# Up products of the first seven expert tiles: plain fp32 from whole copies in place of a high-low split

## The chip, the cores and the metric

One core of one Trainium2 chip runs the whole kernel. The metric is the device time of one execution in microseconds (us). Three runs of the kernel before gave 521.81, 521.89 and 523.43 us; their median, 521.89 us, is what the changed kernel is held against.

## The reference, cut to what matters

A decoder layer over 8 batches of 256 tokens of width 128: causal attention with 16 heads, a retention step, and a mixture of 12 experts of which each token takes 3. The change touches only the experts' up product:

```python
gate_logits = x @ Wg                                  # 12 experts, the 3 largest are taken
h = gelu(einsum('bsd,edh->ebsh', x, Wup) + bup)       # 128 -> 512, this product changes
y = einsum('ebsh,ehd->ebsd', h, Wdown) + bdown        # 512 -> 128
x = x + sum over the 3 chosen experts of weight * y
```

## The kernel before, in words

**Batches.** Attention and retention go batch by batch in a software pipeline over TensorE, VectorE, ScalarE and GpSimd. Each batch's tokens are routed (functions `route_a`, `choose`, `route_b`, `route_c` on VectorE, L1271 to L1318) and GpSimd scatters them by indirect DMA, six transfers of one batch (`send`, L533), into a DRAM table in which every expert owns a region.

**Tiles.** The experts' work is cut into 35 tiles, each for one expert, in one order on every engine. Tiles 0 to 6 (`n < EARLY`) have 256 tokens and are made only of tokens of the first six batches, so they may start before the last batches are routed. Tiles 7 to 23 (up to `BIG`) have 256 tokens and need all batches; tiles 24 to 34 have 128 tokens.

**One tile.** SP loads its rows (`load`, L372 to L388). TensorE transposes them into a PSUM bank (`turn_tokens`, L1034). ScalarE copies the expert's up weights (`up_high`, L761) and the transposed tokens (`tokens_high`, L766). TensorE forms four up products of 128 hidden units each (`up`, L1037 to L1055), ScalarE applies gelu (L746), TensorE forms the down product (`down`, L1074), VectorE adds the bias and scales by the routing weight (`results`, L1512 and L1515), GpSimd scatters the rows (L600).

**The split.** Tiles 0 to 23 take the up product in the type fp32r: ScalarE's copies are the high parts, VectorE forms the low parts of tokens and weights (`tokens`, L1483 and L1496), and each of the four products is three matmuls of 256 columns (`split_product`, L798 to L802: high by high, high by low, low by high). Tiles 24 to 34 take plain fp32 (L1046), with the weights copied by VectorE (L1493) and the tokens by ScalarE. In the profile a plain fp32 matmul stands as two records, an fp32r matmul as one.

**Order around the change.** It is written out by hand. TensorE: `turn(7)` with `turn_tokens(0)` inside it, `weigh(6)`, `counts(6)`, `weigh(7)`, `turn_tokens(1)`, the output projection of the last batch, `up(0)`, two state products, `turn_tokens(2)`, `down(0)`, `up(1)`, two state products, `turn_tokens(3)`, `down(1)`, `up(2)`, the logits of the last batch, `down(2)`, `counts(7)`, and from tile 3 on `turn_tokens(n+1)`, `up(n)`, `down(n-1)`. VectorE has `tokens(0)` between `choose` and the scaling of the attention output (`scale_out`, L1205), then `route_b`, `route_c` of batch 6 and the copy `pad_row` (L1527), and puts `tokens(1)`, `tokens(2)`, `tokens(3)`, `results(0)`, `results(1)` between the steps of the last batch's norms and routing; `late_plan` (L1440) comes after `results(2)`, `small_units` after `results(6)`, `small_rows` after `results(7)`. `turn_tokens(n)` waits until VectorE has both low parts of tile n-1, since they read the same bank.

**SP and GpSimd.** After `pad_row` SP runs a loop of 12 stores (L394 to L396) that write padding rows behind each expert's tokens. GpSimd may scatter the last batch (`begin(7)`, L537 to L542) only when all 12 have landed (`padded`), and SP may load tile 7 (L385 to L388) only when that scatter has landed (`dispatched`). SP's loads of tiles 0 to 5 stand ahead of the padding loop, those from tile 6 on behind it.

Of the kernel before, what the change touches and what calls it, by code (L numbers as in the profile page):

```python
# [12 lines left out]
ACT = mybir.ActivationFunctionType  # L13
AX = mybir.AxisListType

P = 128
# [3 lines left out]
H, DH = 16, 64  # L20
# [4 lines left out]
E, HID, TOPK = 12, 512, 3  # L25
HC = HID // P
N = B * S
SLOTS = 256
# [3 lines left out]
EARLY = -(-((B - 2) * S * TOPK - E * (SLOTS - 1)) // SLOTS)  # L32
SMALL = E - 1
LATE = -(-(UNITS - HALVES * EARLY - SMALL) // HALVES)
BIG = EARLY + LATE
TILES = BIG + SMALL
DEPTH = 6
# [43 lines left out]
def decoder(nc, x, ctx, norm_w, wq, wkv, wout, wg, f_wg, f_wup, f_bup, f_wdown, f_bdown, tables, out):  # L81
    with ExitStack() as stack:
        def sb(name, shape, dt=F32):
            return stack.enter_context(nc.sbuf_tensor(name, shape, dt))
# [4 lines left out]
        def sem(name):  # L89
            return stack.enter_context(nc.semaphore(name))  # L90
# [3 lines left out]
        wq_sb = sb("wq_sb", [P, H * DH])  # L94
# [32 lines left out]
        v_sb = sb("v_sb", [P, T, H, DH])  # L127
# [80 lines left out]
        wup_all = sb("wup_all", [P, E, HID])  # L208
# [13 lines left out]
        wup_hi = sb("wup_hi", [P, 2, HID], F32R)  # L222
        wup_lo = sb("wup_lo", [P, 2, HID], F32R)
        xgT_hi = sb("xgT_hi", [P, 2, SLOTS], F32R)
        xgT_lo = sb("xgT_lo", [P, 2, SLOTS], F32R)
        xg = sb("xg", [P, DEPTH, HALVES, ROW])
        sb("rest_of_early", [P, 512])
        y3 = [a[:, 0:TOPK * FOUT * D].rearrange("p (k n d) -> p k n d", k=TOPK, n=FOUT) for a in (
            wkv_sb, y_in,
            p_sb[:, :, :, :].rearrange("p a h k -> p (a h k)"), pT[:, :, :, :].rearrange("p a h k -> p (a h k)"))]  # L230
# [11 lines left out]
        ffn_up = [[sc[:, 0, :], sc[:, 2, :]], tb]  # L242
        ffn_T = sc[:, 1, :]

        def halves(n):

            return HALVES if n < BIG else 1

        def results_before(n):

            return 16 * sum(halves(m) for m in range(n % DEPTH, n, DEPTH))

        def wup_one(n):

            return v_sb[:, n % 2, 0:HID // DH, :].rearrange("p h d -> p (h d)")

        def xgT_one(n):
            return v_sb[:, n % 2, HID // DH:HID // DH + P // DH, :].rearrange("p h d -> p (h d)")

        def place_of(n):  # L260

            if n < EARLY:
                return first_plan, n
            return (plan, n - EARLY) if n < BIG else (small_plan, n - BIG)
# [17 lines left out]
        def score_place(w, h):  # L282
# [27 lines left out]
        f_T, f_hi, f_w, f_xg, f_up, f_gelu, f_dn, f_y, f_out = (  # L310
            sem(n) for n in ("f_T", "f_hi", "f_w", "f_xg", "f_up", "f_gelu", "f_dn", "f_y", "f_out"))
# [12 lines left out]
        def wait(eng, s, value):  # L324
            if not isinstance(value, int) or value > 0:
                eng.wait_ge(s, value)
# [22 lines left out]
        def _(sp):  # L349
# [22 lines left out]
            def load(n):  # L372
                u = n % DEPTH
                table, k = place_of(n)
                if n >= DEPTH:

                    sp.wait_ge(f_row, n - DEPTH + 1)
                if n - DEPTH >= BIG:
                    sp.wait_ge(f_T, n - DEPTH + 1)
                r = sp.value_load(table[0:1, 0, k:k + 1], min_val=0, max_val=E * CAP)  # L380
                if n == 0:

                    sp.wait_ge(pe_Z, B * PAIRS)
                    sp.wait_ge(dispatched, (1 + (B - 2) * T * TOPK) * 16)
                if n == EARLY:  # L385

                    sp.wait_ge(dispatched, (1 + B * T * TOPK) * 16)
                sp.dma_start(xg[:, u, 0:halves(n), :], xs[bass.ds(r, halves(n) * P), :].rearrange("(a p) w -> p a w", p=P)).then_inc(ld_e[u], 16)  # L388

            sp.wait_ge(v_first, 1)  # L390
            for n in range(DEPTH):
                load(n)
# [4 lines left out]
            for n in range(DEPTH, EARLY):  # L397
                load(n)
# [12 lines left out]
            for c in range(NT // FOUT):  # L411
                for k in range(TOPK):
                    n = slice(c * FOUT, (c + 1) * FOUT)
                    sp.dma_start(y3[c][:, k, :, :], y_v[:, k, n, :]).then_inc(ld_y[c], 16)
            out_v = out.rearrange("b (t p) d -> p (b t) d", p=P)
            for c in range(NT // FOUT):
                n = slice(c * FOUT, (c + 1) * FOUT)
# [206 lines left out]
        def _(act):  # L624
# [113 lines left out]
            expert = {}  # L738
# [11 lines left out]
            def up_high(n):  # L750
                table, k = place_of(n)
                if n == BIG:
                    act.wait_ge(v_plan, 2)
                if n == 0:
                    act.wait_ge(v_first, 1)
                    act.wait_ge(ld_up, 16)
                if n == EARLY:
                    act.wait_ge(v_plan, 1)
                expert[n] = act.value_load(table[0:1, 1, k:k + 1], min_val=0, max_val=E - 1)
                if n < BIG:  # L760
                    act.activation(wup_hi[:, n % 2, :], wup_all[:, bass.ds(expert[n], 1), :].rearrange("p a n -> p (a n)"), ACT.Copy).then_inc(f_w, 1)  # L761

            def tokens_high(n):
                act.wait_ge(f_T, n + 1)
                to = xgT_hi[:, n % 2, :] if n < BIG else xgT_one(n)
                act.activation(to, ffn_T[:, 0:halves(n) * P], ACT.Copy).then_inc(f_hi, 1)  # L766

            def tile(n):
                if n + 1 < TILES:
# [2 lines left out]
                gelu(n)  # L772

            up_high(0)
            tokens_high(0)
            pT_out(B - 1, PAIRS - 1)
# [11 lines left out]
        def _(pe):  # L788
# [9 lines left out]
            def split_product(o, lhs, rhs, last):  # L798

                for n, (l, m) in enumerate(((0, 0), (0, 1), (1, 0))):  # L800
                    ins = pe.matmul(o, lhs[l], rhs[m], start=(n == 0), stop=(last and n == 2), skip_group_check=True)  # L801
                return ins  # L802
# [223 lines left out]
            def turn_tokens(n):  # L1026
                u = n % DEPTH
                pe.wait_ge(ld_e[u], (n // DEPTH + 1) * 16)
                if n > BIG:
                    pe.wait_ge(f_hi, n)  # L1030
                else:
                    wait(pe, f_xg, n)
                for a in range(halves(n)):
                    ins = pe.transpose(ffn_T[:, a * P:(a + 1) * P], xg[:, u, a, 0:D], ident[:, :])  # L1034
                ins.then_inc(f_T, 1)

            def up(n):  # L1037
                pe.wait_ge(f_xg, n + 1)
                if n >= BIG:
                    pe.wait_ge(f_hi, n + 1)  # L1040

                wait(pe, f_gelu, 2 * (n - 1))
                for k in range(HC):
                    c = slice(k * P, (k + 1) * P)
                    if n >= BIG:
                        ins = pe.matmul(ffn_up[n % 2][k // 2][:, (k % 2) * P:(k % 2 + 1) * P], wup_one(n)[:, c], xgT_one(n),  # L1046
                                        start=True, stop=True, skip_group_check=True)
                        if k % 2:
                            ins.then_inc(f_up, 1)
                        continue  # L1050
                    ins = split_product(ffn_up[n % 2][k // 2][:, (k % 2) * SLOTS:(k % 2 + 1) * SLOTS],
                                        (wup_hi[:, n % 2, c], wup_lo[:, n % 2, c]),
                                        (xgT_hi[:, n % 2, :], xgT_lo[:, n % 2, :]), True)
                    if k % 2:
                        ins.then_inc(f_up, 1)  # L1055
# [55 lines left out]
        def _(dve):  # L1111
# [364 lines left out]
            expert = {}  # L1476

            def tokens(n):
                u = n % DEPTH
                table, k = place_of(n)  # L1480
                if n < BIG:
                    dve.wait_ge(f_hi, n + 1)
                    dve.tensor_tensor(xgT_lo[:, n % 2, :], ffn_T[:, 0:SLOTS], xgT_hi[:, n % 2, :], ALU.subtract)  # L1483
                if n == 0:
                    dve.wait_ge(v_first, 1)
                if n == EARLY:
                    dve.wait_ge(v_plan, 1)
                if n == BIG:
                    dve.wait_ge(v_plan, 2)
                expert[n] = dve.value_load(table[0:1, 1, k:k + 1], min_val=0, max_val=E - 1)  # L1490
                if n >= BIG:
                    dve.wait_ge(f_up, 2 * (n - 1))
                    dve.tensor_copy(wup_one(n), wup_all[:, bass.ds(expert[n], 1), :].rearrange("p a n -> p (a n)")).then_inc(f_xg, 1)  # L1493
                else:
                    dve.wait_ge(f_w, n + 1)
                    dve.tensor_tensor(wup_lo[:, n % 2, :], wup_all[:, bass.ds(expert[n], 1), :].rearrange("p a n -> p (a n)"), wup_hi[:, n % 2, :], ALU.subtract).then_inc(f_xg, 1)  # L1496

                if n >= DEPTH:
                    dve.wait_ge(scattered[u], results_before(n))
                a = slice(0, halves(n))  # L1500
                if n >= BIG:
                    dve.wait_ge(ld_e[u], (n // DEPTH + 1) * 16)
                dve.tensor_copy(row_i[:, u, a], xg[:, u, a, D].bitcast(I32))
                dve.tensor_copy(weight[:, u, a], xg[:, u, a, D + 1]).then_inc(f_row, 1)
# [69 lines left out]
            for c in range(NT // FOUT):  # L1574
                dve.wait_ge(ld_y[c], 16 * TOPK)
                n = slice(c * FOUT, (c + 1) * FOUT)
                for k in range(TOPK):
                    ins = dve.tensor_tensor(x_all[:, n, :], x_all[:, n, :], y3[c][:, k, :, :], ALU.add)
# [25 lines left out]
```

## Time and profile before

| what | value |
|---|---|
| median of three runs | 521.89 us (521.81 to 523.43) |
| the profiled execution's own time | 523.74 us |
| its span in the profile | 522.0 us |
[...]
| TensorE busy | 457.5 us, 88% |
| VectorE busy | 393.2 us, 75% |
| ScalarE busy | 329.3 us, 63% |
| GpSimd busy | 256.1 us, 49% |

The profiled execution took 1.74 us around its span (start and end that the profile does not cover). It is 1.85 us above the median of the plain runs and near the highest of them. The expert tiles lie in the last 150 us of the span.

### The profile page before, as it was taken

How to read it: one execution, taken by the hardware profiler on the slowest of the kernel's cores; microseconds unless marked ns; L12 is line 12 of the kernel's file. 1: busy time of each engine (PE TensorE's matmuls, PEld its weight loads, DVE VectorE, ACT ScalarE, POOL GpSimd, SP SyncE). 2: the span in 40 equal slices, each digit the busy share in tenths (PEclk: the TensorE clock that was granted, in tenths of full speed). 3: DMA queues.
4: the chain of work that ended last, by engine and by line, in shares of the span. 5: the costliest groups of instructions: out<-in, count | busy, mean ns of one | idle time of the engine just before them, and what ended most of it. 6: DMA issues, size and time to landing. Idle time of an engine off the chain costs nothing.

```text
span 522.0 us, 12401 instructions
## 1 busy us (share of the span) xinstructions
PE 457.5 (88%) x3540; PEld 374.1 (72%) x3540; DVE 393.2 (75%) x1359; ACT 329.3 (63%) x1001; POOL 256.1 (49%) x398
## 2 busy tenths in 40 slices
PE   1689998999999999999999999976697798999980
PEld 1467786877777678687777767854466688999980
DVE  4755477988888888798888888889688766665556
ACT  3558865875776686687577668643445565776660
POOL 3400005157355535726735653575175764666861
PEclk9989999999999999999999999998798898999995
DMA  8990000000000000000000000001045242222248
GB/s 268 367 225 1 1 0 3 1 16 15 10 7 18 15 0 22 13 5 15 15 10 9 19 12 0 22 17 48 20 143 156 68 107 56 74 71 62 63 112 214
DMA packets 40803, 30.06 MB, mean 58 GB/s; under 512 B 3795, under 2 KB 36999, under 8 KB 40768
## 3 DMA queue, kind: packets, MB, share of 16 engines
q1 hardware_dynamic: 36864, 22.63, 15.5%
q0 software_dynamic: 3472, 6.49, 4.0%
q10 hardware_dynamic: 432, 0.53, 0.4%
q8 instruction: 16, 0.26, 0.2%
q14 instruction: 19, 0.16, 0.1%
HBM read 18.91 MB, written 11.44 MB: 58 GB/s over the span
## 4 chain that ended last, share of the span: by engine, by line
PE 52%; DVE 18%; ACT 8%; issue 8%; SPq 5%; POOL 5%; DMA 3%; DVEq 0%; ACTq 0%; POOLq 0%
PE zb L801 8%; PE sc L840 6%; PE ob L869 6%; PE xb L918 4%; PE zb L1074 3%; PE ob L1074 3%; PE xb L943 3%; PE sc L801 2%; PE tb_a L801 2%; ACT pT L667 2%; PE tb_a L853 2%; PE tb_b L853 2%; PE sc L834 2%; DVE nmx L1187 2%; ACT p_sb L660 2%
## 5 line engine op out<-in xcount | busy, mean ns | idle before, releaser
L651 ACT ACTIVATE qk<-zb 128x512 f32<-128x512 f32 x64 | 38.2, 597 | 66.9 <-PE zb L801 66.9
L520 POOL TENSOR_TENSOR spare_p<-tri 128x1 f32<-128x1 f32 x71 | 14.8, 209 | 125.3 <-DVE xn L1268 67.4
L600 POOL DMA_INDIRECT results_by_token<-y_sb,row_i x59 | 60.3, 1022 | 22.3 <-issue 21.8
L658 ACT ACTIVATE p_sb<-sc,nmx 128x128 f32<-128x128 f32 x128 | 47.1, 368 | 33.9 <-DVE nmx L1187 33.5
L660 ACT ACTIVATE p_sb<-sc,nmx 128x256 f32<-128x256 f32 x128 | 61.0, 476 | 0.0
L840 PE MATMUL sc<-qk 64*128 64x256 f32 (+1 forms) x512 | 60.4, 356 | 0.2 <-ACT qk L651 0.2
L869 PE MATMUL ob<-pT,v_sb 128*64 128x256 f32 (+1 forms) x512 | 58.2, 350 | 1.3 <-DVE oT L1205 1.3
L840 PEld LDWEIGHTS sc<-qk 64*128 64x128 f32 x512 | 45.1, 190 | 15.6 <-issue 10.1
L533 POOL DMA_INDIRECT tokens_by_expert<-packed,slot_i x48 | 48.2, 1005 | 8.6 <-issue 7.4
L1205 DVE TENSOR_TENSOR oT<-ob,pT 128x256 f32<-128x256 f32 x64 | 26.9, 420 | 27.1 <-PE ob L869 27.1
L869 PEld LDWEIGHTS ob<-pT,v_sb 128*64 128x64 f32 x512 | 32.3, 141 | 20.8 <-issue 11.2
L1187 DVE TENSOR_REDUCE nmx<-sc 128x2 f32<-128x512 f32 x64 | 43.5, 680 | 0.0
L1200 DVE TENSOR_TENSOR rg<-rr,gate 128x256 f32<-128x256 f32 x64 | 38.8, 606 | 2.2
L667 ACT ACTIVATE pT<-tb_b 128x512 f32<-128x512 f32 x64 | 39.8, 622 | 0.0
L667 ACT ACTIVATE pT<-tb_a 128x512 f32<-128x512 f32 x64 | 39.1, 612 | 0.0
L801 PE MATMUL zb<-xT_hi,wqk_hi 128*128 128x256 f32 x112 | 36.6, 326 | 1.3 <-ACT xN_hi L639 1.3
L853 PE MATMUL tb_a<-ident,p_sb 128*128 128x128 f32 x192 | 32.0, 276 | 2.2 <-ACT pT L667 2.2
L506 POOL TENSOR_TENSOR sum<-prod 128x256 f32<-128x256 f32 x30 | 21.9, 729 | 24.4 <-DVE prod L1250 24.3
L473 POOL TENSOR_TENSOR kq<-xn,tab 128x256 f32<-128x256 f32 x8 | 5.8, 722 | 55.8 <-DVE xn L1221 55.7
L1074 PE MATMUL zb<-wdn_all,hT 128*128 x248 | 32.3, 285 | 0.7 <-ACT hT L746 0.7
L746 ACT ACTIVATE hT<-sc,bup_sb 128x256 f32<-128x256 f32 (+1 forms) x72 | 25.9, 438 | 10.0 <-PE sc L801 7.8
L853 PE MATMUL tb_b<-ident,p_sb 128*128 128x128 f32 x192 | 31.8, 275 | 0.0
(294 smaller groups left out, 1375.4 us busy)
## 6 DMA issues: line engine op xcount, KB each, us to landing
xg<-tokens_by_expert SPq DMA_DIRECT2D x24, 130.0 KB, 2.2
tokens_by_expert<-padding SPq DMA_DIRECT2D x12, 260.0 KB
wup_all<-in_L_ffn_Wup SPq DMA_DIRECT2D x1, 3072.0 KB, 14.4
wdn_all<-in_L_ffn_Wdown SPq DMA_DIRECT2D x12, 256.0 KB, 5.7
wkv_sb<-in_L_attn_Wkv SPq DMA_DIRECT2D x2, 512.0 KB, 6.5
ctx_b<-in_ctx SPq DMA_DIRECT2D x8, 128.0 KB, 2.1
out<-x_all SPq DMA_DIRECT2D x4, 256.0 KB, 3.3
results_by_token<-y_sb,row_i POOLq DMA_INDIRECT x59
```

Source lines behind the costliest of these rows:

```text
L533: pool.indirect_dma_start(out=xs, out_offset=bass.IndirectOffsetOnAxis(ap=slot_i[:, t, k:k + 1], axis=0), in_=packed[:, t, k, :], in_offse ...
L600: pool.indirect_dma_start(out=ys, out_offset=bass.IndirectOffsetOnAxis(ap=row_i[:, u, a:a + 1], axis=0), in_=y_sb[:, u, a, :], in_offset=None,
L658: act.activation(p_sb[:, w, h, 0:P], sc[:, k, S:S + P], ACT.Exp, bias=nmx[:, w, 0, n:n + 1], accum_out=total[:, w, 0, h:h + 1])
L660: act.activation(p_sb[:, w, h, P:3 * P], sc[:, k, 0:S], ACT.Exp, bias=nmx[:, w, 1, n:n + 1], accum_out=total[:, w, 1, h:h + 1]).then_inc(a ...
L667: ins = act.activation(pT[:, s % 2, h, :], tb[h][:, :], ACT.Copy)
L801: ins = pe.matmul(o, lhs[l], rhs[m], start=(n == 0), stop=(last and n == 2), skip_group_check=True)
L840: ins = pe.matmul(sc[:, score_bank(w, h), o:o + n], qk[r, 0, t * P:(t + 1) * P], qk[r, 1, 0:n], start=False, stop=(t == 0), skip_group_che ...
L853: pe.transpose(tb[h][:, k * P:(k + 1) * P], p_sb[:, s % 2, h, k * P:(k + 1) * P], ident[:, :])
L869: ins = pe.matmul(ob[h * DH:(h + 1) * DH, t * P:S], v_sb[:, t, 2 * s + h, :], pT[:, s % 2, h, t * S:(2 + t) * P], start=(t == 0), stop=(t ...
L1074: ins = pe.matmul(ffn_out(n)[:, a * D:(a + 1) * D], hT[:, n % 2, k, a * P:(a + 1) * P], wdn_all[:, bass.ds(e, 1), k, :].rearrange("p a d - ...
L1187: dve.tensor_reduce(nmx[:, w, 1, :], sc[:, w:w + 2, 0:S], AX.X, ALU.max, negate=True).then_inc(v_nm, 1)
L1200: dve.tensor_tensor(rg[:, s % 2, :, :].rearrange("p t (h d) -> p t h d", h=2), bc(rr[:, :, :], 3, DH), bc(gate[:, :, 2 * s:2 * s + 2], 3, ...
```

## The change

The seven early tiles take their up product as the small tiles do: one plain fp32 matmul for each block of 128 hidden units, with 256 token columns. ScalarE's two copies go to whole fp32 buffers: the weights to `wup_full`, which lies in the attention's `wq_sb`, the tokens to `xgT_full`, a new buffer in the place of an unused one. VectorE's two subtractions of these tiles are gone, and with them its waits for `f_hi` and `f_w`; `tokens(n)` of an early tile now waits for the tile's load itself. `turn_tokens(n)` waits, for a previous tile that is plain, for ScalarE's copy of the tokens. SP's loads of tiles 6 to 12 wait also for the transposes of the tile whose buffer they take. The small tiles use the new buffers too; the 17 tiles between keep the split.

```diff
-        sb("rest_of_early", [P, 512])
+        xgT_full = sb("xgT_full", [P, 2, SLOTS])
...
+        def plain(n):
+            return n < EARLY or n >= BIG
+        def wup_full(n):
+            return wq_sb[:, n % 2 * HID:(n % 2 + 1) * HID]
...
             def load(n):
-                if n - DEPTH >= BIG:
+                if n >= DEPTH and plain(n - DEPTH):
                     sp.wait_ge(f_T, n - DEPTH + 1)
...
             def up_high(n):
-                    act.activation(wup_hi[:, n % 2, :], wup_all[...], ACT.Copy).then_inc(f_w, 1)
+                    act.activation(wup_full(n) if plain(n) else wup_hi[:, n % 2, :], wup_all[...], ACT.Copy).then_inc(f_w, 1)
             def tokens_high(n):
                 act.wait_ge(f_T, n + 1)
-                to = xgT_hi[:, n % 2, :] if n < BIG else xgT_one(n)
-                act.activation(to, ffn_T[:, 0:halves(n) * P], ACT.Copy).then_inc(f_hi, 1)
+                to = xgT_full if plain(n) else xgT_hi
+                act.activation(to[:, n % 2, 0:halves(n) * P], ffn_T[:, 0:halves(n) * P], ACT.Copy).then_inc(f_hi, 1)
...
             def turn_tokens(n):
-                if n > BIG:
+                if n and plain(n - 1):
                     pe.wait_ge(f_hi, n)
-                else:
-                    wait(pe, f_xg, n)
+                elif n:
+                    pe.wait_ge(f_xg, n - EARLY)
...
             def up(n):
-                pe.wait_ge(f_xg, n + 1)
-                if n >= BIG:
+                if n >= EARLY:
+                    pe.wait_ge(f_xg, n + 1 - EARLY)
+                if n < EARLY:
+                    pe.wait_ge(f_w, n + 1)
+                if plain(n):
                     pe.wait_ge(f_hi, n + 1)
...
-                    if n >= BIG:
-                        ins = pe.matmul(ffn_up[n % 2][k // 2][:, (k % 2) * P:(k % 2 + 1) * P], wup_one(n)[:, c], xgT_one(n),
+                    if plain(n):
+                        w = halves(n) * P
+                        ins = pe.matmul(ffn_up[n % 2][k // 2][:, (k % 2) * w:(k % 2 + 1) * w], wup_full(n)[:, c], xgT_full[:, n % 2, 0:w],
...
             def tokens(n):
-                if n < BIG:
+                if not plain(n):
                     dve.wait_ge(f_hi, n + 1)
                     dve.tensor_tensor(xgT_lo[:, n % 2, :], ffn_T[:, 0:SLOTS], xgT_hi[:, n % 2, :], ALU.subtract)
...
-                else:
+                elif n >= EARLY:
                     dve.wait_ge(f_w, n + 1)
                     dve.tensor_tensor(wup_lo[:, n % 2, :], wup_all[...], wup_hi[:, n % 2, :], ALU.subtract).then_inc(f_xg, 1)
...
-                if n >= BIG:
+                if plain(n):
                     dve.wait_ge(ld_e[u], (n // DEPTH + 1) * 16)
```

## Rows read from the trace of the kernel before

**Rows 1.** The profile page: span, granted clock in 40 slices

```profile
span 522.0 us, 12401 instructions
...
PEclk9989999999999999999999999998798898999995
```

**Rows 2.** Chain that ended last, 366 to 430: start us, us, what

```profile
370.56 0.42 DVE xgT_lo L1483
...
371.62 0.69 DVE wup_lo L1496
...
372.46 0.34 DVE oT L1205
...
372.94 1.56 PE ob L869 x8
...
377.35 0.20 DVE pad_row L1527
...
401.95 3.01 DMA tokens_by_expert<-padding
405.02 0.19 POOL spare_p L520
...
414.85 2.35 DMA xg<-tokens_by_expert
...
417.69 1.44 PE sc L801 x12
419.12 1.79 PE zb L1074 x16
```

**Rows 3.** Timeline of all engines, 366 to 406: start us, us, what, idle before

```profile
369.90 1.55 PE L869 MATMUL ob<-pT,v_sb 128*64 128x256 f32 x8
...
370.10 0.17 DVE L1289 TENSOR_SCALAR hit<-rep 128x24 f32<-128x24 f32 x1
...
381.10 1.02 PE L937 MATMUL xb<-wkv_sb,tri 128*128 128x512 f32 x2
...
381.95 1.02 PE L937 MATMUL ob<-wkv_sb,tri 128*128 128x512 f32 x2
...
385.30 14.96 SPq L396 DMA_DIRECT2D tokens_by_expert<-padding  x8
...
404.19 0.23 DVE L1317 TENSOR_REDUCE packed<-samew 128x6 f32<-128x72 f32 x1
```

**Rows 4.** The same timeline, TensorE's waits for tiles 5, 6 and 7

```profile
406.12 0.41 PE L1034 MATMUL sc<-ident,xg 128*128 128x128 f32 x2 [2.82 <-DVE wup_lo L1496]
...
412.53 0.41 PE L1034 MATMUL sc<-ident,xg 128*128 128x128 f32 x2 [1.20 <-DVE wup_lo L1496]
...
417.25 0.44 PE L1034 MATMUL sc<-ident,xg 128*128 128x128 f32 x2 [1.08 <-DMA xg<-tokens_by_expert]
```

**Rows 5.** The chain from 434 on: one tile's set, twice, and a small tile's products

```profile
434.55 0.56 PE sc L1034 x2
435.12 2.56 PE sc L801 x12
437.68 2.04 PE zb L1074 x16
439.72 0.22 PE sc L1034 x2
...
443.15 0.22 PE sc L1034 x2
...
484.35 0.89 PE sc L1046 x8
```

**Rows 6.** Stretches: us, PE, PEld, DVE, ACT, POOL busy (x), PEclk, DMA share, GB/s

```profile
404.00:406.00 2.00, 0.00 (x0) 0.00 (x0) 1.60 (x8) 2.00 (x5) 0.83 (x2) 1.00 0.35 67
...
408.00:411.00 3.00, 3.00 (x17) 3.00 (x17) 2.69 (x12) 1.69 (x4) 2.16 (x3) 0.54 0.14 44
...
435.00:438.00 3.00, 3.00 (x16) 3.00 (x16) 2.37 (x15) 1.41 (x4) 1.62 (x3) 0.50 0.27 72
```

More of the change, by code:

```diff
@@ L251, in results_before @@
             return 16 * sum(halves(m) for m in range(n % DEPTH, n, DEPTH))
[L253 to L258, printed above, removed]
+        def plain(n):
+            return n < EARLY or n >= BIG
+        def wup_full(n):
+            return wq_sb[:, n % 2 * HID:(n % 2 + 1) * HID]
         def place_of(n):
@@ L760, in up_high @@
                 if n < BIG:
-                    act.activation(wup_hi[:, n % 2, :], wup_all[:, bass.ds(expert[n], 1), :].rearrange("p a n -> p (a n)"), ACT.Copy).then_inc(f_w, 1)
+                    act.activation(wup_full(n) if plain(n) else wup_hi[:, n % 2, :], wup_all[:, bass.ds(expert[n], 1), :].rearrange("p a n -> p (a n)"), ACT.Copy).then_inc(f_w, 1)
             def tokens_high(n):
                 act.wait_ge(f_T, n + 1)
-                to = xgT_hi[:, n % 2, :] if n < BIG else xgT_one(n)
-                act.activation(to, ffn_T[:, 0:halves(n) * P], ACT.Copy).then_inc(f_hi, 1)
+                to = xgT_full if plain(n) else xgT_hi
+                act.activation(to[:, n % 2, 0:halves(n) * P], ffn_T[:, 0:halves(n) * P], ACT.Copy).then_inc(f_hi, 1)
             def tile(n):
@@ L1492, in tokens @@
                     dve.wait_ge(f_up, 2 * (n - 1))
-                    dve.tensor_copy(wup_one(n), wup_all[:, bass.ds(expert[n], 1), :].rearrange("p a n -> p (a n)")).then_inc(f_xg, 1)
-                else:
+                    dve.tensor_copy(wup_full(n), wup_all[:, bass.ds(expert[n], 1), :].rearrange("p a n -> p (a n)")).then_inc(f_xg, 1)
+                elif n >= EARLY:
                     dve.wait_ge(f_w, n + 1)
```

## The prediction, made before the changed kernel was seen

> **What bounds the kernel now.** I read the page first, for the span and for the slices in which the granted clock is below full [rows 1]: they lie in the stretch in which the last batch and the early expert tiles run together. Then the chain that ended last through that stretch [rows 2]. It does not run through the early tiles. It runs through VectorE's work for tile 0 (the low part of the tokens, the low part of the weights, then the scaling `oT`), through the last attention product on TensorE (PE ob L869), back to VectorE until `pad_row` at 377.35, and from there through SP's loop of 12 padding stores, the last of which starts at 401.95. Eight of the stores take 14.96 us [rows 3]: the loop goes by SP's own pace of about 2 us a store. When they have landed GpSimd may go on (405.02), it scatters the last batch, SP loads tile 7 (2.35 us, from 414.85), and at 417.25 TensorE turns tile 7 [rows 2, 4]. From there the chain is TensorE without a gap: the up product of tile 6 (1.44 us), a down product (1.79 us), and so on [rows 2]. The timeline shows what TensorE does in front of that point [rows 4]: it waits 2.82 us and 1.20 us for VectorE's low part of the weights, and 1.08 us for the load of tile 7. So tiles 0 to 6 have slack, 5.1 us in these three waits alone, and tile 7 has none.
>
> **What is removed.** From VectorE two subtractions for each of seven tiles: 0.42 + 0.69 = 1.11 us a tile [rows 2], 7.8 us in all. What counts is where they lie.
>
> *Tile 0* lies on the chain. `choose` ends at 370.27 (370.10 + 0.17), and the attention product that `oT` reads ends at 371.45 (369.90 + 1.55) [rows 3]. Without the subtractions VectorE still has a register load and two small copies, for which there is room until about 371.5. So `oT` starts at about 371.5 in place of 372.37, where the two copies let it start now (0.1 us ahead of its row in the chain) [rows 2]. All that follows on the chain moves by the same amount, up to tile 7: **-0.85 us**, with bounds of -1.1 (the whole subtraction time) and -0.4 (if the register load, now behind the subtraction, holds `oT` up).
>
> *Tiles 1 to 6* lie beside the padding loop. Their cover is SP's loop and the scatter, 377.35 to 417.25. The routing of the last batch, through which they could matter, gave its slots at 404.42 (404.19 + 0.23), 0.5 us ahead of the padding's landing [rows 2, 3]. After the change the landing moves to about 404.1; routing loses three tiles' subtractions, 3.3 us, ahead of it, though part of that turns into waiting for the state products. It stays ahead. I price these six at 0. If that cover were gone they would be worth up to the 2.82 + 1.20 us of the waits.
>
> **What is added.** TensorE takes four plain fp32 products of 256 columns in place of 12 fp32r ones, which take 1.44 us [rows 2]. There is no row of this shape. From one side: a plain fp32 product of 512 columns takes 0.85 us from its start to the next one's (381.10 to 381.95) [rows 3], so half of it four times is 1.70 us. From the other: four products of 128 columns take 0.89 us [rows 5], twice that is 1.78. I take 1.76, **+0.32 us** a tile. Six of the seven are in slack. The product of tile 6 is queued behind the transposes of tile 7 and so on the chain: +0.32 counts once (bounds +0.26 and +0.34).
>
> **What is moved.** ScalarE does the same two copies of each tile, to other buffers: 0. `turn_tokens(n)` of tiles 1 to 7 waits for ScalarE's copy in place of VectorE's low parts; that ends 2.82 and 1.20 us of waiting [rows 4], and what is late next is the load of tile 7. No DMA and no GpSimd instruction is added. SP waits in addition, for the loads of tiles 6 to 12, until the transposes of a tile six places earlier are done. Behind that wait stand all later loads, and TensorE waits for them; but these loads are issued after 402 and from tile 7 on after 414.85 [rows 2], when those transposes are over: 0. The small tiles only change buffers: 0.
>
> **The clock.** Here is the cost. TensorE's slack now gathers in one place. The three waits together are 5.1 us; the three products of tiles 3 to 5 take 1.0 of it and the earlier tile 7 takes 0.85, so at least 3.3 us of idleness stand right in front of tile 7, and up to 6 if the early tiles start sooner too. [...] The price: one tile's set (two transposes, 12 up and 16 down products) took 434.55 to 439.72 = 5.17 us in a slow stretch and 439.72 to 443.15 = 3.43 us after it [rows 5], so **+1.74 us**. Below, it could be 0 (no fall); above, the longest stretch of two such prices, 3.5.
>
> [...]
>
> **Sum.** -0.85 + 0.32 + 1.74 = +1.2 us. The profiled execution took 523.74 us, 1.85 above the median; one slow stretch more or less (1.74) would explain that, and it has one at 435 on the chain. Against the median the sum gives 521.89 + 1.21 = **523.1 us**; against the profiled execution 524.95.
>
> **The rivals.** What a measurement can tell here from no change is 0.3%, 1.6 us.
>
> *A, no slow stretch on the chain.* For it: a wait of 1.20 us left the clock full, and the fall at 408 came late. Against it: the idle time will be longer than any in these rows. 521.89 - 0.85 + 0.32 = 521.4 us. If moreover tile 0's wait doesn't go (the register load holds `oT`), 521.8. Chance 0.22; within 0.3%.
>
> *B, slower: the slow stretch at tile 7 and another behind the planning on VectorE.* The chain after tile 8 goes over VectorE's planning, and TensorE idles before 434.55; the profiled execution was slow there [rows 5, 6] and I take the median run not to be. If the restart is slow and that stretch falls slow too, the two prices add: 523.1 + 1.74 = 524.8 us. It decides as soon as both gaps let the clock fall. Chance 0.28, slower.
>
> *C, faster: VectorE's time is worth something.* If the padding were not what holds the last batch's scatter but its routing, tile 7 would follow VectorE, and the waits of 2.82 and 1.20 us would be won: 521.4 - 4.0 = 517.4, or 520 for part of it. Against it: the two landings at 404.42 and 404.96 stand the wrong way round, and the first moves more. Chance 0.10, faster.
>
> *The forecast*, one slow stretch: chance 0.40, own range 522.4 to 523.8; seven tenths of it lie below 523.46 (0.28 within 0.3%, 0.12 slower).
>
> **How the numbers follow.** Faster 0.10; within 0.3%: 0.22 + 0.28 = 0.50; slower 0.28 + 0.12 = 0.40. The range takes in A with its larger gain (521.4 - 0.25, rounded down for a little of C: 520.9) and B (524.8): 520.9 to 524.8, leaving out most of C and a doubly slow restart.
>
> **What would show it.** In the profile after: `oT` about 371.5 and `pad_row` about 376.5 (tile 0's step); twelve stores at the old pace; TensorE's transposes of tile 7 at about 416.4, released by the load's DMA, with over 3 us of idle time ahead of them (now 1.08); L1483 and L1496 with 17 instances each; the up product of tile 6 in eight records over 1.76 us, or 3.5 us at the low clock; a granted clock near 0.5 in the stretch from 416 on. I am wrong if tile 7 turns clearly earlier than 416, if the idle time before it is short, or if the clock stays full behind it.

## The result

The changed kernel takes 524.2 us (median of 17 runs, 523.09 to 526.83), the kernel before 522.25 us (17 runs, 519.55 to 524.35). The ratio is 1.0046, with a 95% interval of 1.0029 to 1.0063: slower by 2 us, an interval clear of 1. The profiled execution took 524.31 us, close to the median.

**The page of the changed kernel.** The lines that answer to [rows 1]: the span and the granted clock in 40 slices.

```profile
span 522.5 us, 12332 instructions
...
PEclk9999999999999999999999999997898798999995
```

The slices say little here, since only their place changed, and the mean granted clock is 0.966 against 0.965 in the profile before. The chain does.

**The chain that ended last, after** (start us, us, what; line numbers are a few higher than before). It answers to [rows 2].

```profile
375.22 0.20 DVE pad_row L1532
...
399.87 3.04 DMA tokens_by_expert<-padding
402.98 0.22 POOL spare_p L521
...
412.19 2.19 DMA xg<-tokens_by_expert
414.43 0.69 PE sc L1035 x2
415.12 3.41 PE sc L1051 x8
418.53 1.83 PE zb L1079 x16
420.36 0.22 PE sc L1035 x2
```

The same links in the same order: VectorE to `pad_row`, SP's padding stores, GpSimd's scatter, the load, tile 7. Everything up to tile 7 is earlier than before, and tile 6's up product takes 3.41 us where it took 1.44. VectorE did lose work of the early tiles: its routing of the last batch was ready 32.40 us after the last `rg` (a VectorE instruction of the last attention step, L1200 before), against 35.38 before, but the padding, landed 34.73 us after it, still released the scatter.

**TensorE's waits for early and late tiles, after**, from the timeline (idle time before it and its releaser in brackets). They answer to [rows 4].

```profile
404.16 0.38 PE L1035 MATMUL sc<-ident,xg 128*128 128x128 f32 x2
...
414.43 0.69 PE L1035 MATMUL sc<-ident,xg 128*128 128x128 f32 x2 [6.37 <-DMA xg<-tokens_by_expert]
...
428.40 0.41 PE L1035 MATMUL sc<-ident,xg 128*128 128x128 f32 x2 [1.16 <-DVE wup_lo L1501]
...
434.36 0.41 PE L1035 MATMUL sc<-ident,xg 128*128 128x128 f32 x2 [2.33 <-DVE wup_lo L1501]
```

The first row is tile 6's, which now starts without a wait. The waits for VectorE's low parts, 2.82 and 1.20 us, are gone. In their place stands one wait of 6.37 us for the load of tile 7.

**Stretches, after** (us; busy PE, PEld, DVE, ACT, POOL with counts; granted clock; DMA share; GB/s). They answer to [rows 6].

```profile
408.00:411.00 3.00, 0.06 (x1) 0.00 (x0) 1.79 (x8) 0.46 (x1) 2.32 (x4) 1.00 0.14 46
411.00:415.00 4.00, 0.57 (x3) 0.57 (x4) 0.00 (x0) 0.00 (x0) 3.23 (x4) 0.58 0.42 109
415.00:417.00 2.00, 2.00 (x6) 1.60 (x6) 1.10 (x3) 0.42 (x2) 1.74 (x3) 0.50 0.51 146
417.00:420.00 3.00, 3.00 (x19) 2.69 (x18) 0.16 (x3) 2.14 (x5) 1.86 (x2) 0.75 0.52 119
420.00:424.00 4.00, 4.00 (x38) 4.00 (x37) 2.13 (x8) 2.54 (x7) 1.57 (x3) 1.00 0.33 91
...
435.00:438.00 3.00, 3.00 (x19) 3.00 (x18) 2.18 (x15) 2.29 (x6) 1.81 (x3) 0.59 0.24 66
```

TensorE is empty from 408.06 to 414.43. The granted clock falls while it is empty: it is 1.00 until 411.7 and 0.50 from there to 418.5, through tile 7's transposes and tile 6's product, then 1.00 again. The last row, behind the planning, is a slow stretch that the kernel before has too (0.50 in [rows 6]).

**Where the difference between the two profiles lies.** The two executions reach the last attention steps at different times, so I count from the start of the last `rg` on VectorE (369.05 before, 368.18 after), and from one tile's transposes on TensorE to the next's:

| section | before | after | difference |
|---|---|---|---|
| last `rg` to `pad_row` | 8.30 | 7.04 | -1.26 |
| `pad_row` to tile 7's transposes | 39.90 | 39.21 | -0.69 |
| tile 7's transposes to tile 8's | 3.50 | 5.77 | +2.27 |
| tile 8's to tile 10's | 8.19 | 8.20 | 0 |
| tile 10's to tile 11's | 5.61 | 5.96 | +0.35 |
| tile 11's to the last tile's | 67.97 | 68.02 | +0.05 |
| the last tile's to the end | 19.48 | 20.12 | +0.64 |

The span is 0.5 us longer: these sum to +1.36, and the last `rg` was 0.87 earlier. The medians differ by 1.95. The profile of the kernel before was one of its longer runs (523.74 against 522.25), and the first two rows hold luck in its disfavour. In the first, the last attention product ran in 0.87 us after, at a granted clock of 1.00 (from 370.7 on), and in 1.55 us before, at 0.50 (369.8 to 376.6); the experiments below take that out. In the second, from GpSimd's release (`spare_p`) to tile 7's transposes it took 12.23 us before and 11.45 us after; the same stretch takes 11.46 and 11.47 us in the profiles of the changed kernel again and of its second filler run, so the 0.69 us is mostly a scatter that was slow in this one profile. The last row can't be read either: that stretch, which no edit touches, takes between 18.4 and 20.2 us in the 14 profiles of this case.

### The profile page after: what moved, and what is told of

It reads as the page before. It is cut to its first block, busy times and chain, and to the rows that moved or that the text cites. A ratio compares the mean times of both kernels' runs of the same rounds, so it can differ in the third digit from the quotient of the medians.

```text
span 522.5 us, 12332 instructions
## 1 busy us (share of the span) xinstructions
PE 460.8 (88%) x3512; PEld 376.2 (72%) x3512; DVE 387.1 (74%) x1345; ACT 329.1 (63%) x1001; POOL 253.8 (49%) x398
## 4 chain that ended last, share of the span: by engine, by line
PE 52%; DVE 17%; ACT 9%; issue 8%; SPq 5%; POOL 5%; DMA 3%; DVEq 0%; POOLq 0%; ACTq 0%
PE zb L802 8%; PE sc L841 6%; PE ob L870 6%; PE xb L919 4%; PE zb L1079 4%; PE ob L1079 3%; ACT pT L668 3%; PE xb L944 3%; PE tb_a L854 2%; PE tb_a L802 2%; PE tb_b L854 2%; ACT p_sb L661 2%; ACT p_sb L659 2%; PE sc L835 2%; PE sc L802 2%
## 5 line engine op out<-in xcount | busy, mean ns | idle before, releaser
L601 POOL DMA_INDIRECT results_by_token<-y_sb,row_i x59 | 59.8, 1013 | 22.3 <-issue 22.1
L870 PE MATMUL ob<-pT,v_sb 128*64 128x256 f32 (+1 forms) x512 | 57.1, 345 | 0.4 <-DVE oT L1210 0.4
L802 PE MATMUL zb<-xT_hi,wqk_lo 128*128 128x256 f32 x112 | 32.0, 286 | 0.0
```

Of the source, the lines that this page charges most:

```text
L601: pool.indirect_dma_start(out=ys, out_offset=bass.IndirectOffsetOnAxis(ap=row_i[:, u, a:a + 1], axis=0), in_=y_sb[:, u, a, :], in_offset=None,
L870: ins = pe.matmul(ob[h * DH:(h + 1) * DH, t * P:S], v_sb[:, t, 2 * s + h, :], pT[:, s % 2, h, t * S:(2 + t) * P], start=(t == 0), stop=(t ...
```

## The experiments

Theory 1: tile 0 gives some 0.85 us, the other six early tiles give nothing because they stand beside SP's padding stores, and their freed time gathers in one gap in front of tile 7, which costs clock. Theory 2: the plain products or the moved waits cost the time, and the clock is incidental.

Each kernel ran twelve times, in one of four sets with the kernel before beside it, each set on another chip. In the first two sets the kernel before took 534.8 and 534.9 us, some 12 us more than elsewhere, with stalls on several engines that no wait of the program explains, so from them the profiles' sections are used more than the times. In the last two sets it took 522.1 and 521.7.

**Filler matmuls in the gap.** Six of them, 5.1 us of work whose result nothing reads, before `turn_tokens(7)`:

```diff
+                if n == EARLY - 1:
+                    pe.wait_ge(v_filled, B + 1)
+                    for _ in range(6):
+                        pe.matmul(xb[:, :], ident[:, :], wdn_all[:, 0, :, :]..., start=True, stop=True)
                 if n + 1 < TILES:
                     turn_tokens(n + 1)
```

> The changed kernel with six extra fp32 matmuls of 512 columns (5.1 us of work whose result nothing reads) on TensorE just before it turns tile 7, in the 6.4 us in which it now idles. Theory 1 (the idle time costs clock): the transposes of tile 7 stay at about 414.4, the product of tile 6 takes 1.8 us in place of 3.6 us, the time falls from 524.2 by 1.7 us to about 522.5. Theory 2 (the plain fp32 products or the moved waits cost the time, the clock is incidental): 524.2, unchanged.

534.06 us, ratio 0.9969 (0.9938 to 1.0001), against 1.0010 (0.9977 to 1.0043) for the changed kernel in another set of the same pace. The product of tile 6 took 1.89 us and tile 7's transposes to tile 8's 3.73 us, at a granted clock of 1.00 (402.6 to 436.8). Two stalls of 0.41 and 0.44 us fell among the fillers, and tile 7 turned right behind them, 49.45 us after `rg` against 47.48 in the changed kernel of a set of that pace: here the filler itself held tile 7 up. The intervals of the times overlap, so the same kernel was run again in a set of the usual pace.

> The changed kernel with six filler matmuls, again, because the run's times could not be told from those of the kernel before. Theory 1 (idle time costs clock): tile 6's product and tile 5's down product together take 3.7 us between the transposes of tiles 7 and 8, against 5.8 and 6.0 us in two profiles of the changed kernel; ratio to before 0.996 to 1.001. Theory 2 (clock incidental): 5.8 us again, ratio 1.001 to 1.0046.

522.54 us, ratio 1.0005 (0.9986 to 1.0024). This interval and that of the changed kernel (1.0029 to 1.0063) don't meet. The timeline of TensorE in that kernel (L1110 is the filler):

```profile
410.31 5.32 PE L1110 MATMUL xb<-wdn_all,ident 128*128 128x512 f32 x12
416.79 0.44 PE L1035 MATMUL sc<-ident,xg 128*128 128x128 f32 x2 [1.16 <-DMA xg<-tokens_by_expert]
417.06 1.89 PE L1051 MATMUL sc<-xgT_full,wq_sb 128*128 128x256 f32 x8
418.79 1.95 PE L1079 MATMUL zb<-wdn_all,hT 128*128 x16
420.57 0.38 PE L1035 MATMUL sc<-ident,xg 128*128 128x128 f32 x2
```

and its stretches behind tile 7:

```profile
415.00:418.00 3.00, 1.84 (x9) 1.11 (x8) 0.32 (x1) 0.38 (x1) 2.54 (x4) 1.00 0.58 155
418.00:421.00 3.00, 3.00 (x25) 2.90 (x24) 1.05 (x5) 2.23 (x6) 2.53 (x4) 1.00 0.52 120
```

The granted clock is 1.00 in both stretches, and 416.79 to 420.57 is 3.78 us in place of 5.77. The product, the waits and the order are those of the changed kernel, but for the fillers and one wait in front of them that was long over. In this section that is theory 1 and excludes theory 2. Between the two ratios lie 0.41%, 2.1 us, by which the useless work makes the kernel faster. The times alone show this less firmly than the section: the two ratios come from different sets, the gap between their intervals is 0.0005, and the interval here still reaches into the range 1.001 to 1.0046 that I had given theory 2. The median granted clock of all runs points the same way: 0.969 with fillers, 0.966 for the kernel before in the same set, 0.966 for the changed kernel in the runs of the result.

**Five fillers, one fewer.**

> The changed kernel with five extra fp32 matmuls of 512 columns (4.3 us) ahead of tile 7's transposes, one fewer than in the earlier run so that they end before the load lands. Theory 1 (the idle time costs clock): 1.7 us below the changed kernel of this set, ratio to before about 1.001; the product of tile 6 in 1.8 us. Theory 2 (the clock is incidental): ratio as the changed kernel's.

533.55 us, ratio 0.9995 (0.9961 to 1.0030). In the same set the changed kernel has 1.0010 (0.9977 to 1.0043): the right order, but overlapping intervals. At tile 7 the granted clock was 1.00 (402.0 to 419.0), but in this profile TensorE stalled inside the product of tile 6:

```profile
416.81 0.60 PE L1051 MATMUL sc<-xgT_full,wq_sb 128*128 128x256 f32 x2
418.30 0.59 PE L1051 MATMUL sc<-xgT_full,wq_sb 128*128 128x256 f32 x2 [0.89 <-issue]
419.74 1.86 PE L1051 MATMUL sc<-xgT_full,wq_sb 128*128 128x256 f32 x4 [0.85 <-issue]
```

"issue" is idle time that no semaphore or DMA in the profile explains; 1.7 us went in it, and the last four records ran at 0.50 again (419.1 to 422.5). Such stalls stand in the profiles of both slower sets. No run shows where they come from, and this time says nothing about the change.

**The yardstick in the same set.**

> The changed kernel itself, as the yardstick on the chip of this set. Both theories: about 1.0045 of the kernel before, tile 7 turned behind more than 4 us of idle time, the product of tile 6 in about 3.6 us.

535.47 us, ratio 1.0010 (0.9977 to 1.0043): the ratio missed the expected 1.0045 though its interval almost reaches it. The shape held: 5.71 us of idle time ahead of tile 7, the product in 3.62 us at a granted clock of 0.50 (414.2 to 421.1), 6.03 us from tile 7's transposes to tile 8's.

**Only tile 0 plain, and only tile 0 split.** Both by changing which tiles `plain(n)` names, with the counts of the waits. The diff is that of the first; the second names `(1, 2, 3, 4, 5, 6)` in place of `(0,)`.

```diff
         def plain(n):
-            return n < EARLY or n >= BIG
+            return n in (0,) or n >= BIG
```

> Only tile 0 takes the plain product; tiles 1 to 6 keep the split. Theory 1: the chain keeps tile 0's gain (pad_row about 0.85 us earlier against the steps before it), TensorE keeps its short waits for VectorE's low parts and the wait for tile 7's load stays near 1 to 2 us, so no long gap and no extra slow stretch: 522.25 - 0.85 = 521.4 us. Theory 2 (tile 0's subtractions were hidden and the change has only costs): 522.3.

534.84 us, ratio 0.9992 (0.9964 to 1.0019).

> The changed kernel with tile 0 split again, tiles 1 to 6 plain. Theory 1: tile 7 turns about 0.85 us later against the steps before it, the idle gap ahead of it is still over 5 us and the product of tile 6 still slow: 524.2 + 0.85 = 525.0 us. Theory 2: no gain from tile 0, so 524.2.

535.84 us, ratio 1.0009 (0.9979 to 1.0040). By the times neither theory is told from the other. With only tile 0 plain, 0.9984 (theory 1) and 1 both lie in the interval. With only tile 0 split, the ratio is below both expected ones (525.0 and 524.2 us of 522.25: 1.0053 and 1.0037), the first of them outside the interval; but in the slower sets the changed kernel itself has 1.0010 and not 1.0046. The profiles tell more. Tile 7's transposes with only tile 0 plain, and with only tile 0 split:

```profile
418.57 0.41 PE L1039 MATMUL sc<-ident,xg 128*128 128x128 f32 x2 [1.45 <-DVE wup_lo L1505]
```

```profile
415.89 0.69 PE L1039 MATMUL sc<-ident,xg 128*128 128x128 f32 x2 [5.04 <-DMA xg<-tokens_by_expert]
416.38 3.62 PE L1055 MATMUL sc<-xgT_full,wq_sb 128*128 128x256 f32 x8
```

With tiles 1 to 6 split the wait is 1.45 us and the section to tile 8 is 3.46 us, at a granted clock of 1.00 (409.7 to 437.0); with them plain the gap is 5.04 us and the section 6.46 us, at 0.50 (414.6 to 421.4). So the gap comes from tiles 1 to 6, and the slow section with it (a part of these 6.46 us is a stall like those above, since the changed kernel took 5.77). And tile 0's own worth can be read from the last `rg` to `pad_row`, if only profiles with the same clock in that section are compared:

| the two last attention products | tile 0 split | tile 0 plain |
|---|---|---|
| both slow, the transposes of `rg` ahead of them at full clock | 8.30 (before) | 7.43 ("all of it", below), 7.36 (changed kernel again) |
| both slow, these transposes slow too | no profile | 7.67 (only tile 0), 7.68 (filler again) |
| both fast (0.87 us) | 7.65 (tile 0 split), 7.62 (written out, split) | 6.63 (tile 6 split), 6.62 (five fillers) |

"Slow" is 1.50 to 1.55 us for a product, at a granted clock of 0.50 (but for 0.2 us or less), and "fast" is at 1.00; the first transpose of `rg` takes 0.33 us in the first row and 0.47 us in the second. Tile 0 is worth 0.9 us at 0.50 and 1.0 us at 1.00. The second row has no partner and can't be set against 8.30: there the first product itself starts 0.25 us later (1.10 us after `rg` in place of 0.85).

**Tile 6 alone split again.**

> The changed kernel with tile 6 alone split again. The gap ahead of tile 7 stays, since VectorE does tile 6's low parts inside it. Theory 1: the product of tile 6 takes twelve short matmuls at the low clock, about 2.9 us in place of 3.5; 0.6 us below the changed kernel. Theory 2 (plain products cost more than their count of columns says): more than 1.5 us below it.

535.89 us, ratio 1.0021 (0.9994 to 1.0047), not below the changed kernel's 1.0010. The twelve short matmuls stood 417.37 to 420.90, 3.5 us at a granted clock of 0.50 (416.1 to 426.3) with a stall of 0.29 us in it, and tile 5's down product began at 421.33, after 0.43 us of waiting for ScalarE's `hT`. The 0.6 us was not seen, and neither was the 1.5 us of theory 2.

**Tile 6's product ahead of tile 7's transposes.**

```diff
             for n in range(LAST_CHAIN, TILES):
+                if n == EARLY - 1:
+                    up(n)
                 if n + 1 < TILES:
                     turn_tokens(n + 1)
-                up(n)
+                if n != EARLY - 1:
+                    up(n)
```

> The changed kernel with the up product of tile 6 queued ahead of the transposes of tile 7, so that it runs in the idle gap. Theory 1: behind the gap TensorE begins with the transposes of tile 7 and the down product of tile 5 at the low clock; one product of 1.76 us at full clock leaves the chain, so 524.2 - 1.8 = 522.4 us, and still a slow stretch behind 414. Theory 2 (TensorE is not the chain behind tile 7; VectorE's preparation of tile 7 is): no more than 0.5 us, 523.7.

535.70 us, ratio 0.9993 (0.9959 to 1.0027), an interval with 1 and the changed kernel's 1.0010 in it. The profiled execution took 538.98 us, with ScalarE idle for 13.15 us across tile 7's transposes, so its section behind tile 7 isn't read.

**The padding stores written out.** This tests the cover: whether SP's stores hold tile 7.

```diff
-            with sp.Fori(0, E) as i:
-                r = sp.value_load(pad_row[0:1, bass.ds(i, 1)], min_val=0, max_val=E * CAP - PAD)
+            for i in range(E):
+                r = sp.value_load(pad_row[0:1, i:i + 1], min_val=0, max_val=E * CAP - PAD)
```

> The changed kernel with SP's twelve padding stores written out in place of the loop, the same stores. If SP's pace is what holds tile 7: a store takes less than 2.1 us, the padding lands earlier, until the last batch's routing is what GpSimd waits for; tile 7 turns up to 2.8 us earlier, the gap ahead of it shrinks from 6.4 to about 3.6 us, and the time falls by 2 to 4.5 us below the changed kernel. If the DMA engines set the pace of the stores: nothing changes.

533.53 us, ratio 0.9962 (0.9926 to 0.9999), against 1.0010 (0.9977 to 1.0043) for the changed kernel in the set: about 2.5 us less, with overlapping intervals. The stores took 14.92 us in place of 23.50, VectorE's routing was the releaser in place of the padding, and the gap shrank to 3.97 us. But the release came 34.24 us after `rg` and tile 7 turned 46.26 us after it, against 47.48 us in the changed kernel of this set and 46.25 us in that of the result: 1.2 us or nothing, where up to 2.8 had been expected. VectorE's routing took some 2 us longer there than in the result's profile (19.35 against 17.25 us from `prod` to `packed`).

> SP's padding stores written out, all early tiles split as before the change. In the earlier run the twelve stores took 14.9 us in place of 23.5 and GpSimd's scatter of the last batch was then released by VectorE's routing. If that holds, VectorE's subtractions are now on the chain: the scatter starts 2 us or more later, counted from the last rg of the attention, than with plain early tiles (34.2 us there), and the kernel is slower than the written-out plain one by about that, ratio to before 0.998 to 1.000. If routing is not what holds the scatter, it starts at the same distance, 34 us.

521.93 us, ratio 0.9998 (0.9978 to 1.0017).

> SP's padding stores written out, plain early tiles, and the up product of tile 6 queued ahead of tile 7's transposes. Both gains add if each is real: tile 7 turns at the written-out kernel's distance, and one product (1.76 us at full clock, up to 3.5 at the low one) leaves the chain behind it. Ratio to before 0.992 to 0.995. If behind tile 7 VectorE's low parts and not TensorE are the chain, the second gain is missing: 0.996.

521.83 us, ratio 0.9972 (0.9941 to 1.0003), with runs from 517.47 to 526.15: an interval that just reaches 1, and a gain smaller than expected (0.992 to 0.995). GpSimd's release for the last batch and SP's stores in the split and in the plain kernel, both written out:

```profile
403.92 0.20 POOL L525 TENSOR_TENSOR spare_p<-tri 128x1 f32<-128x1 f32 x1 [1.53 <-DVE packed L1326]
...
377.00 14.13 SPq L401 DMA_DIRECT2D tokens_by_expert<-padding  x12
```

```profile
401.95 0.20 POOL L521 TENSOR_TENSOR spare_p<-tri 128x1 f32<-128x1 f32 x1 [0.55 <-DVE packed L1325]
...
377.63 14.20 SPq L397 DMA_DIRECT2D tokens_by_expert<-padding  x12
...
413.82 0.44 PE L1035 MATMUL sc<-ident,xg 128*128 128x128 f32 x2 [2.99 <-DMA xg<-tokens_by_expert]
414.68 2.99 PE L1079 MATMUL zb<-wdn_all,hT 128*128 x16 [0.43 <-issue]
417.47 0.63 PE L1035 MATMUL sc<-ident,xg 128*128 128x128 f32 x2
```

Now VectorE's routing (`packed`) is what GpSimd waits for, and there the plain tiles pay: counted from the last `rg`, the release comes at 35.50 us with split tiles and at 31.89 us with plain ones (before 35.97, after 34.80, both released by the padding). Not all of these 3.6 us is the change. The output projection of the last batch, on which VectorE waits, ran at two clocks:

```profile
374.13 5.39 PE L923 MATMUL xb<-wout_sb,oT 128*128 128x128 f32 x32 [0.58 <-DVE filled L1306]
```

```profile
374.76 3.81 PE L919 MATMUL xb<-wout_sb,oT 128*128 128x128 f32 x32 [0.58 <-DVE filled L1305]
```

The first is the split kernel (granted clock 0.50 from 374.0 to 377.4), the second the plain one (1.00 from 372 to 379). That is 1.6 us of luck, and 2.0 us are left for the subtractions. Tile 7 turned 43.76 us after `rg`, against 48.20 before. In this kernel too the clock fell, 1.7 us behind the gap of 2.99 us: it was 0.50 from 415.6 to 419.0, and tile 5's down product took 2.99 us.

**All of it, with three fillers in the smaller gap.**

> Written-out padding stores, plain early tiles, tile 6's up product queued ahead of tile 7's transposes, and three filler matmuls (2.6 us) in the remaining gap of 3 us. If the three findings add: the scatter of the last batch is released by routing, 32 us after the last rg; tile 7 turns 43.8 us after it; tile 5's down product behind it takes 1.95 us at full clock in place of 2.99 us. Against the written-out kernel with tile 6 first about 1 us less; ratio to before 0.990 to 0.996. If the filler is late it holds tile 7 up instead, and the ratio is 0.996 to 0.999.

522.59 us, ratio 1.0008 (0.9985 to 1.0031): the gains did not add. The filler did its part (a granted clock of 1.00 from 381.7 to 436.3, tile 5's down product in 2.05 us, 2.75 us from tile 7's transposes to tile 8's in place of 3.65). What failed is the part before it: GpSimd's release came 35.43 us after `rg` in place of 31.89, and tile 7 turned 47.3 us after it. GpSimd and the output projection in this kernel:

```profile
404.71 0.24 POOL L521 TENSOR_TENSOR spare_p<-tri 128x1 f32<-128x1 f32 x1 [2.94 <-DMA tokens_by_expert<-packed,slot_i]
404.88 1.03 POOL L529 COPY packed<-xn 128x384 f32<-128x384 f32 x2
406.08 0.20 POOL L521 TENSOR_TENSOR spare_p<-tri 128x1 f32<-128x1 f32 x1 [0.17 <-POOL packed L529]
...
376.16 6.46 PE L919 MATMUL xb<-wout_sb,oT 128*128 128x128 f32 x32 [0.33 <-DVE filled L1309]
```

GpSimd packs the last batch only when the scatter of the batch before has landed. Its last transfer was issued at 397.35 and released this wait at 404.71, 7.4 us later. But that is not what was lost: in the kernel with the gain the same transfer was issued at 393.34 and released the same wait at 400.21, 6.9 us later. What differs is the clock. It stood at 0.50 through the last attention products and nearly all of the output projection (371.5 to 381.7; 1.00 from 371.2 on in the other profile), so that `pad_row` came 7.43 us after `rg` in place of 6.62 and the projection took 6.46 us in place of 3.81. VectorE's next step came 3.45 us later for it, which is nearly all of the 3.54 us. These two profiles therefore don't say whether the gains would add at the same clock; the times say that over twelve runs they did not show.

Only the written-out plain kernel has an interval that stays below 1 (0.9926 to 0.9999), by 0.0001 and in a set with stalls; no kernel here is firmly faster than the one before.

## Why the prediction was right

The forecast was 523.1 us with a range of 520.9 to 524.8; 524.2 lies in it, with the ratio on the slower side, for which I had given 0.40. The likeliest class, within 0.3%, was missed: +0.46% measured, +0.23% forecast.

*What bounds the kernel* held: the chain after has the same links. *Tile 0*: -0.85 forecast, -0.9 or -1.0 measured, by the clock of the attention products beside it. The step "`oT` starts when the product it reads ends" was right: 2.45 us after `rg` was foreseen, and it is 2.43 and 2.44 us in the two profiles whose clock there stood as before (the changed kernel again, and all of it). *Tiles 1 to 6 at 0*: right; the padding still released the scatter (4.25 us of waiting on GpSimd ahead of 402.98). *The plain product*: +0.32 forecast; with the filler, tile 7's transposes to tile 8's take 3.78 us against 3.50, so +0.28. *The moved waits*: right, both gone, and next late was the load of tile 7.

*The clock*: right in place, and the fillers bear out the cause: with them in the gap the granted clock is 1.00 and the slow stretch at tile 7 is gone. The gap was foreseen at 3.3 to 6 us and is 6.37. That a gap of this length brings a slow stretch was my estimate, from the idle and the slow stretches of [rows 6]. The term was mis-sized: +1.74 forecast, while 5.77 - 3.78 = 1.99 us in the profile and 2.1 us between the medians' ratios (1.0046 - 1.0005 of 522). The price was taken from tile 11's set [rows 5], whose transposes had begun when the clock fell (they took 0.56 us) and in which the clock was 0.50 for 3.4 us (434.7 to 438.1). Here it was 0.50 from 411.7 on, the transposes of tile 7 took 0.69 us, and it stayed at 0.50 until 418.5, 4.1 us of tile 7's section. If half of the time at 0.50 is lost, these are 1.7 and 2.0 us, which is an estimate of mine and close to the 1.74 and 1.99. Where the fall comes differs between the two profiles: before, it came at 407.4, 1.3 us after tile 6's transposes had begun, and the clock was 1.00 from 411 to 417, around the wait of 1.20 us; after, it came 2.8 us ahead of tile 7's transposes, so that these began at 0.50.

*Rival A* (no slow stretch, 521.4) is excluded by the granted clock of 0.50. *Rival B* (a second slow stretch behind the planning, 524.8): the profiles before and after both have one there, at 435 to 438 (0.50 and 0.59), so it is no difference between them; that the median run of before lacks it was my assumption, and 11 of the 14 profiles of this case have a slow stretch at tile 11. *Rival C*'s condition was false here (routing 32.40 us after `rg`, padding 34.73), but the written-out kernels show that it was the right condition: with the padding out of the way the release follows VectorE, by 2.0 of the 3.6 us between two profiles.

*What no step had*: 0.35 us between tiles 10 and 11. The terms as measured are tile 0 (-0.9), the product (+0.28), the clock (+1.99) and this (+0.35): +1.7 us, against +1.95 us between the medians (interval 1.5 to 3.3). Without the clock they give -0.3 us, and the filler kernel measured +0.3 us (interval -0.7 to +1.3). The forecast of +1.2 us is lower than the sum because the clock's price was 0.25 us too small and the 0.35 us were not in it.

*A sign of being wrong that did occur*: I had written that I would be wrong if tile 7 turned clearly earlier than 416, and it turned at 414.43. Of these 2.8 us against before, 0.87 us lie ahead of `rg`, 0.9 us are tile 0, and 0.4 and 0.7 us are the luck in the first two rows of the table. Counted from `rg`, tile 7 turned at 47.48 us in the changed kernel's second profile and at 48.20 before, 0.7 us earlier where 0.85 was forecast. An absolute time was a poor sign, since the whole execution shifts.

## What to carry to other kernels

When an edit removes work beside the chain, ask where the freed time will stand. Here waits of 2.82, 1.20 and 1.08 us gave way to one of 6.37 us in front of work that is on the chain; the granted clock fell from 1.00 to 0.50 in it, and the chain paid 2.0 us. A stage is worth what it is worth only where its cover ends: here the first tile (0.9 to 1.0 us) and none of the next six. To test whether a slowdown is clock and not work, fill the gap with work that nothing reads: product, waits and order stay, and here the clock alone changed (1.00 in place of 0.50 behind tile 7, the section 3.78 us in place of 5.77).

## What had not been expected

**A stall without a wait.** Between tiles 10 and 11 VectorE goes through the last step of the plan to tile 11's low parts. In the changed kernel the chain has, in this place:

```profile
432.91 0.06 DVEq L1495
432.96 0.39 issue
433.35 0.02 DVEq L1495
```

and in the kernel before:

```profile
433.45 0.06 DVEq L1490
433.50 0.03 issue
433.54 0.02 DVEq L1490
```

The instructions and their waits are the same. TensorE's wait behind it is 2.33 us in place of 1.98. It is 2.33 to 2.35 us in the changed kernel (twice), both kernels with six fillers, the three with tile 6's product first and the written-out plain one, and 1.98 to 2.00 in the kernels with tile 0 split (before, tile 0 split, written out split) and in that with tile 6 split. Two profiles of the slower sets stand apart: 3.48 us with only tile 0 plain, 3.23 us with five fillers. What sets it is open; among the others it goes with the program, not with the run.

**The loop's price, and what the DMAs take back.** SP issues twelve stores in 23.5 us from a loop and in 14.2 us written out: 2.0 and 1.2 us a store, for the same DMAs. The landings gain less. From the loop (second filler profile) a store lands 2.7 to 5.0 us after its issue; written out (split kernel) the second lands after 3.5 us and the twelfth after 8.3, later with each one. The scatters issued beside them are slower too: the last two of batch 6 land 5.5 and 4.8 us after issue, against 3.1 and 3.5 before. So from the first issue to the last landing it is 22.1 us in place of 26.8, a gain of 4.7 us and not of 9.

**The clock ahead of the change.** The stretch around the last attention products is slow or fast from run to run of kernels that don't differ there (for an attention product 1.55 us at a granted clock of 0.50 or 0.87 us at 1.00; for the output projection 3.81 us at 1.00 and 6.46 us with 0.50 in all but its last 0.9 us). So two of these profiles can only be compared section by section, at the same clock.
